# Output projections of the first two tiles start earlier, and the work at the seam of two phases is put in another order

## The reference

```
x = x + layernorm(attention(layernorm(x)))        # causal, 16 heads of 64, rotary on q and k
x = x + layernorm(ffn(layernorm(x)))
attention: q, k, v = x Wq, x Wk, x Wv ; out = softmax(mask(q k^T) / 8) v ; out Wo
ffn:       scores = 8 softmax(x Wr^T + br) ; low = x A^T (8 experts, rank 16)
           out = 2 * sum over experts of scores * (low B^T)
```

## Time and profile before

| | us |
|---|---|
| median of three runs | 1061.37 |
| lowest and highest of the runs | 1061.04, 1061.68 |
| the profiled execution, own time | 1061.38 |
| its span, first to last instruction | 1059.6 |
| mean granted TensorE clock, share of full speed | 0.997 |
| busy: PE, DVE, ACT, POOL | 1037.3, 753.5, 624.0, 421.5 |

### The profile page before, as it was taken

How to read it: one execution, slowest core, us unless ns; L and a number is a source line. 1 busy time by engine, 2 the same in 40 slices (tenths; PEclk the granted TensorE clock), 3 DMA queues, 4 the chain that set the end, 5 groups by cost and what they waited for, 6 DMA issues and landing times.

```text
span 1059.6 us, 19431 instructions
## 1 busy us (share of the span) xinstructions
PE 1037.3 (98%) x6135; PEld 897.5 (85%) x6135; DVE 753.5 (71%) x2170; ACT 624.0 (59%) x1454; POOL 421.5 (40%) x422
## 2 busy tenths in 40 slices
PE   7999999999999999999999999999989999999996
PEld 6988888888888888888888888888877888888884
DVE  8576777777676667667766766676766777777777
ACT  7567666767665666566665756666685333333334
POOL 5143524443362536245342624444367232333221
PEclk9999999999999999999999999999999999999999
DMA  7013323331320247011111101110342323332311
GB/s 298 21 65 110 110 71 110 110 110 51 96 73 27 92 161 249 21 51 50 55 51 50 54 13 51 51 51 16 100 159 62 119 81 100 119 104 88 105 61 60
DMA packets 58699, 90.83 MB, mean 86 GB/s; under 512 B 3568, under 2 KB 36336, under 8 KB 58608
## 3 DMA queue, kind: packets, MB, share of 16 engines
q1 hardware_dynamic: 58464, 89.44, 26.3%
q10 hardware_dynamic: 144, 0.26, 0.1%
HBM read 64.52 MB, written 25.17 MB: 85 GB/s over the span
## 4 chain that ended last, share of the span: by engine, by line
PE 80%; DVE 6%; ACT 5%; issue 5%; POOL 1%; DVEq 0%; ACTq 0%; POOLq 0%
PE bank L1523 26%; PE bank L1468 24%; PE bank L1550 14%; PE bank L1582 5%; PE bank L1602 3%; PE bank L1601 2%; PE bank L1720 2%; PE bank L1697 1%; DVE prob L1121 1%; ACT prob L805 1%; ACT q_hl L826 1%; PE bank L1721 1%; ACT xin L787 1%; ACT pT L816 1%; ACT xn L769 1%
## 5 line engine op out<-in xcount | busy, mean ns | idle before, releaser
L653 POOL TENSOR_SCALAR prob<-prob,rinv 128x128 f32<-128x128 f32 (+3 forms) x256 | 137.5, 537 | 442.2 <-DVE rinv L1131 442.2
L805 ACT ACTIVATE prob<-prob,nmax 128x128 f32<-128x128 f32 (+3 forms) x256 | 144.3, 564 | 231.9 <-DVE nmax L1121 230.0
L1523 PE MATMUL bank<-big_hi,w_hi 128*128 128x512 f32 (+1 forms) x520 | 217.2, 418 | 0.6 <-DVE big_lo L1096 0.3
L1523 PE MATMUL bank<-big_hi,w_lo 128*128 128x512 f32 (+1 forms) x520 | 203.3, 391 | 0.0
L1523 PE MATMUL bank<-big_lo,w_hi 128*128 128x512 f32 (+1 forms) x520 | 202.3, 389 | 0.0
L1121 DVE CUSTOM_DVE_ANT_0 prob<-bank,mask 128x256 f32<-128x256 f32 (+2 forms) x192 | 106.2, 553 | 64.5 <-PE bank L1468 63.2
L1550 PE MATMUL bank<-wv_hi,big_hi 128*128 128x256 f32 x512 | 132.9, 293 | 0.0
L1550 PE MATMUL bank<-wv_hi,big_lo 128*128 128x256 f32 x512 | 127.2, 281 | 0.0
L1139 DVE TENSOR_TENSOR pT<-bank,pT 128x128 fp32r<-128x128 f32 (+3 forms) x256 | 124.3, 486 | 1.6 <-ACT pT L816 1.4
L1582 PE MATMUL bank<-ident,prob 128*128 128x128 f32 x640 | 111.9, 273 | 5.2 <-DVE pT L1139 3.4
L1523 PEld LDWEIGHTS bank<-big_hi,w_lo 128*128 128x128 f32 x520 | 97.6, 188 | 21.6
(11 more groups left out here) (159 smaller groups left out, 2281.0 us busy)
## 6 DMA issues: line engine op xcount, KB each, us to landing
w_raw<-in_wqkv SPq DMA_DIRECT2D x32, 512.0 KB, 4.5
wv_raw<-in_wqkv SPq DMA_DIRECT2D x16, 512.0 KB, 4.5
attention_out<-o_sum SPq DMA_DIRECT2D x64, 128.0 KB, 2.3
w_raw<-attention_out SPq DMA_DIRECT2D x16, 512.0 KB, 4.8
land<-in_x SPq DMA_DIRECT2D x16, 512.0 KB, 3.7
out<-res SPq DMA_DIRECT2D x14, 512.0 KB, 2.7
xin<-in_x SPq DMA_DIRECT2D x12, 512.0 KB, 4.0
xT_hold_hi<-xin SPq DMA_DIRECT2D x8, 512.0 KB, 3.6
```

What stands on the lines that cost most here:

```text
L653: pool.tensor_scalar(p, p, rinv[:, q % 4:q % 4 + 1], 1.0, ALU.mult, ALU.mult).then_inc(prob_done, 1)
L805: act.activation(prob[:, q % 4, 0:n], prob[:, q % 4, 0:n], ACT.Exp, scale=-1.0, bias=nmax[:, q % 4:q % 4 + 1], accum_out=rsum[:, q % 4:q % ...
L1523: done = pe.matmul(grp_ps[k][:, cols], w, xt[:, cols], start=at == 0, stop=at == GROUP_MM - 1)
```

## The change

- The chunks of tile 0 begin two steps earlier (`Y_FIRST_AT`: slot 31, step 6), and tile 1 begins in slot 32, step 6 instead of slot 33, step 0; twelve of its chunks instead of eight stand inside the slots. Half 0 of tile 1 goes to the bank `tr_ps`, which the v projections used (`y_bank`), and the transposes of the first half of tile 0 to `sc_ps[0]`. The waits follow the banks.
- ScalarE: `oT_high(0)` a step later, Wo chunk 4 a step later and chunk 5 two steps later, `oT_high(2)` a step later, the first `ln_start` of tile 0 two steps earlier, the second ahead of the last `o_lower`.
- GpSimd: `oT_low(0)` a step later; Wo chunks 5, 6 and 7 a step earlier; `oT_low(1)` two steps earlier; `bt_lo` behind `chunk_sums`. In all slots, the first `w_pairs` moves from step 1 of the odd slot to step 3 of the even slot ahead of it, and `wv_low` comes a step earlier.
- VectorE: `y_variance(0)` moves from slot 33, step 1 to slot 32, step 7, ahead of the last `negate`; the first sums and statistics of x1 from step 3 to step 2; the low part of the second half of tile 0 ahead of the copy of the column sums.
- TensorE: `columns` moves behind the first chunk of tile 2.

```
--- before.py
+++ after.py
...
 CHUNKS = 8
-Y_FIRST = (((0, 0), (0, 1), (0, 2)), ((0, 3), (0, 4)), ((1, 0), (1, 1)), ((1, 2), (1, 3)), ((1, 4), (0, 5)),
-           ((1, 5),), ((0, 6), (1, 6)), ((0, 7), (1, 7)))
-Y_SECOND = ((0, 1), (2, 3, 4), (5, 6, 7))
+Y_FIRST = (((0, 0), (0, 1)), ((0, 2), (0, 3)),
+           ((1, 0), (1, 1), (1, 2)), ((1, 3), (0, 4)), ((1, 4), (0, 5)), ((1, 5), (0, 6)), ((1, 6),), ((0, 7), (1, 7)))
+Y_SECOND = (((0, 0), (0, 1)), ((0, 2), (0, 3)), ((0, 4), (0, 5)), ((0, 6), (0, 7), (1, 0)), ((1, 1), (1, 2), (1, 3)))
 WO_EARLY = UPH - 2
 WO_SLOT = STEPS * (UNITS - 2)
-WO_AT = {STEPS * WO_EARLY + 4: 0} | {WO_SLOT + s: c for s, c in ((4, 1), (9, 2), (10, 3), (12, 4), (13, 5), (16, 6), (17, 7))}
-WO_POOL_AT = {STEPS * WO_EARLY + 6: 0} | {WO_SLOT + s: c for s, c in ((6, 1), (9, 2), (10, 3), (13, 4), (16, 5), (17, 6), (18, 7))}
+Y_FIRST_AT = STEPS * UNITS - 2
+Y_SECOND_AT = Y_FIRST_AT + len(Y_FIRST)
+WO_AT = {STEPS * WO_EARLY + 4: 0} | {WO_SLOT + s: c for s, c in ((4, 1), (9, 2), (10, 3), (13, 4), (15, 5), (16, 6), (17, 7))}
+WO_POOL_AT = {STEPS * WO_EARLY + 6: 0} | {WO_SLOT + s: c for s, c in ((6, 1), (9, 2), (10, 3), (13, 4), (15, 5), (16, 6), (17, 7))}
 EARLY = TILES // 2
...
-            if isinstance(t, int) and t == 0 and k == 1:
-                return pt_ps[0]
+            if isinstance(t, int) and t == 0:
+                return pt_ps[0] if k == 1 else sc_ps[0]
             return grp_ps[0] if final(t) and k == 1 else tr_ps
+
+        def y_bank(t, i, k):
+
+            return tr_ps if isinstance(t, int) and t == 1 and k == 0 else y_ps[i][k]
...
                     divide(u, s)
-                    if u % QUAD == QUAD - 1 and u < UNITS - 1 and s in (3, 4):
-                        wv_low(u // QUAD + 1, s - 3)
-                    if b == 1 and not (isinstance(u, int) and u >= UNITS - 1):
-                        if s in (1, 6):
-                            w_pairs(s // 6, n + 1)
+                    if u % QUAD == QUAD - 1 and u < UNITS - 1 and s in (2, 3):
+                        wv_low(u // QUAD + 1, s - 2)
+                    if b == 0 and u < UNITS - 2 and s == 3:
+                        w_pairs(0, n + 1)
+                    if b == 1 and u < UNITS - 1:
+                        if s == 6:
+                            w_pairs(1, n + 1)
                         if s in (5, 7):
                             w_low(s // 7, n + 1)
-                    if isinstance(u, int) and STEPS * u + s == STEPS * UNITS - 5:
+                    if u == UNITS - 1 and s == 4:
                         oT_low(0, 0)
-                    if isinstance(u, int) and u == UNITS and s in (4, 5):
-                        oT_low(1, 1, PART * (s - 4), PART * (s - 3))
+                    if u == UNITS and s in (2, 3):
+                        oT_low(1, 1, PART * (s - 2), PART * (s - 1))
                     if isinstance(u, int) and u == UNITS + 1 and s == 2:
                         oT_low(2, 0)
-                    if isinstance(u, int) and u == UNITS + 1 and s == 3:
-                        pool.wait_ge(bt_hi_done, 1)
-                        pool.tensor_tensor(bt_lo, bt_raw, bt_hi.bitcast(F32), ALU.subtract).then_inc(bt_lo_done, 1)
                     if isinstance(u, int) and STEPS * u + s in WO_POOL_AT:
...
             chunk_sums()
+            pool.wait_ge(bt_hi_done, 1)
+            pool.tensor_tensor(bt_lo, bt_raw, bt_hi.bitcast(F32), ALU.subtract).then_inc(bt_lo_done, 1)
             for t in range(2, 6):
...
                         x_normal(ahead_tile(u) + 1)
-                    if isinstance(u, int) and u == UNITS - 1 and s in (3, 6):
-
+                    if u == UNITS - 1 and s in (4, 6):
                         act.wait_ge(grp_done, 2 * u + s // 3)
...
                     if isinstance(u, int) and u == UNITS + 1:
-                        if s == 1:
+                        if s == 2:
                             oT_high(2, 0, 32)
-                        if s == 2:
+                        if s == 0:
                             ln_start(ln_first(0))
...
                             act.activation(ar_hi, ar_raw[:, :, :], ACT.Copy).then_inc(ffn_hi_done, 1)
+                            ln_start(ln_second(0))
                             o_lower(u - 2, 1)
-                        if s == 4:
-                            ln_start(ln_second(0))
                     if isinstance(u, int) and u == UNITS and s == 5:
...
                         hold_chunk(u, HOLD_AT.index(s), half, ahead)
+                    if u == UNITS and s == 7:
+                        y_variance(0, 0)
                     if isinstance(u, int) and u == UNITS + 1:
-                        if s == 1:
-                            y_variance(0, 0)
-                        if s == 3:
-                            dve.memset(br_sb[:, 0:HR], 0.0).then_inc(br_zeroed, 1)
-                            dve.memset(ones[:, :], 1.0).then_inc(ones_set, 1)
+                        if s == 2:
                             y_scale(0, 0)
...
                             ln_variance(ln_second(0))
+                        if s == 3:
+                            dve.memset(br_sb[:, 0:HR], 0.0).then_inc(br_zeroed, 1)
+                            dve.memset(ones[:, :], 1.0).then_inc(ones_set, 1)
                             o_add(u - 2, 1)
...
                         dve.wait_ge(res_done, t - 1)
-                dve.scalar_tensor_tensor(out=x1_of(t, i)[:, half(k)], in0=y_ps[i][k][:, :], scalar=rs1[:, 0:1],
+                dve.scalar_tensor_tensor(out=x1_of(t, i)[:, half(k)], in0=y_bank(t, i, k)[:, :], scalar=rs1[:, 0:1],
                                          in1=xres[:, i, half(k)], op0=ALU.mult, op1=ALU.add
...
             x2T_low(0, 0)
+            x2T_low(0, 1)
+            dve.wait_ge(y0_done, 1)
+            half_stats(0, y_bank(1, 1, 0)[:, :])
             dve.wait_ge(col_done, 1)
...
             low_base(0)
-            x2T_low(0, 1)
-            dve.wait_ge(y0_done, 1)
-            half_stats(0, y_ps[1][0][:, :])
             for t in range(2, 6):
...
                     if isinstance(t, int) and t == 0:
-                        pe.wait_ge(rot_done, 2 * UNITS)
+                        pe.wait_ge(rot_done, 2 * UNITS - 1)
                     pe.wait_ge(oT_hi_done, t + 1)
...
                     if isinstance(t, int) and t == 1:
-                        pe.wait_ge(neg_done, STEPS * UNITS - 1)
+                        pe.wait_ge(v_hi_done, 2 * UNITS)
+                        pe.wait_ge(v_lo_done, 2 * UNITS)
                     if late(t, 2):
                         pe.wait_ge(x1_done, t - 1)
+                if isinstance(t, int) and t == 0 and k == 1 and c0 == 0:
+                    pe.wait_ge(rot_done, 2 * UNITS)
                 if isinstance(t, int) and t == 1 and k == 1 and c0 == 0:
...
                     cols = slice(512 * k, 512 * k + 512)
-                    last = products(y_ps[i][k][:, :], [(oT_hi[:, i, c, :], wo_hi[c][:, cols]),
+                    last = products(y_bank(t, i, k)[:, :], [(oT_hi[:, i, c, :], wo_hi[c][:, cols]),
                                                        (oT_lo[:, i, c, :], wo_hi[c][:, cols]),
...
-                    if isinstance(u, int) and STEPS * u + s in range(STEPS * UNITS, STEPS * UNITS + len(Y_FIRST)):
-                        for k, c in Y_FIRST[STEPS * (u - UNITS) + s]:
+                    if STEPS * u + s in range(Y_FIRST_AT, Y_SECOND_AT):
+                        for k, c in Y_FIRST[STEPS * u + s - Y_FIRST_AT]:
                             y_half(0, 0, k, c, c + 1)
-                    if isinstance(u, int) and u == UNITS + 1 and s < len(Y_SECOND):
-                        for c in Y_SECOND[s]:
-                            y_half(1, 1, 0, c, c + 1)
+                    if STEPS * u + s in range(Y_SECOND_AT, Y_SECOND_AT + len(Y_SECOND)):
+                        for k, c in Y_SECOND[STEPS * u + s - Y_SECOND_AT]:
+                            y_half(1, 1, k, c, c + 1)
...
                 if isinstance(t, int) and t == 0 and k == 0:
-                    pe.wait_ge(v_hi_done, 2 * UNITS)
-                    pe.wait_ge(v_lo_done, 2 * UNITS)
+                    pe.wait_ge(neg_done, STEPS * UNITS)
                 elif isinstance(t, int) and t == 0:
...
                 y_half(t, i, 0, 0, 1)
+                if isinstance(t, int) and t == 2:
+                    columns()
                 low_rank(t - 2)
...
-            y_half(1, 1, 1, 0, 4)
+            y_half(1, 1, 1, 4, 6)
             x2_turn(0, 0, 0)
-            y_half(1, 1, 1, 4, 6)
-            columns()
+            y_half(1, 1, 1, 6, 7)
             x2_turn(0, 0, 1)
-            y_half(1, 1, 1, 6, KC)
+            y_half(1, 1, 1, 7, KC)
             for t in range(2, 6):
...
```

## The result

The changed kernel takes 1064.73 us (median; 1064.28 to 1066.09), the kernel before 1061.37 (1061.04 to 1061.68): ratio 1.0035, 95% interval 1.0025 to 1.0045. It is slower, by 3.4 us. The forecast was 1062.6, the range 1058.4 to 1065.4. The time lies inside the range, but outside the forecast's own narrower one (1061.2 to 1063.8): what came is the second rival on top of the forecast, at 1064.8.

What follows compares the result with a forecast made beforehand. TensorE was taken as the bound (busy 1037 of 1060 us), VectorE's chain close behind. Gains in slot 31 are given back in four waits, `low_turn` comes later: 1061.4 + 1.3 = 1062.6 us, rounded; range 1058.4 to 1065.4.

Steps and rivals of the forecast that it cites:

- second rival: Behind `oT_low(2)`, `bt_lo` comes first and blocks `ar_lo`, which ends 2.2 us later: 1064.8 us; chance 0.24.
- sum of +1.3 us: At the first `low_turn`: it starts at 830.8 against 829.47, and the delay is carried to the end.
- Slot 31: Four chunks of tile 0 fill the 2.17 us gap after a 0.8 us wait; later transposes start at 786.5, not 786.09.
- Slots 0 to 30 at nothing (-0.3 to +0.5): Moving `w_pairs` and `wv_low` there stays within GpSimd's idle share: 0 us, range -0.3 to +0.5.
- GpSimd in slot 32: `divide` queues behind `wo_low(5)`; TensorE waits 1.6 and 1.4 us, and item 1's transposes start 2.0 us later.
- VectorE's order: `y_variance` (1.7 us) ahead of the last `negate`, which starts 3.1 us late; VectorE is free for x1 1.7 us late.
- a race: After the last `pt_low`, `bt_lo` starts 5.6 us behind it and `ar_lo` is ready 5.7 us behind it.
- a fall of the clock in slot 32: Gaps of 1.6, 0.6 and 0.8 us there bring half speed, costing 1.7 us: 1064.3 us; chance 0.08.
- To the end: Behind `low_turn` the order of turns is unchanged, so the 1.3 us is carried to the end.
- Rival 1: In slots 31 and 32 the divisions keep ahead of TensorE and the lead survives: 1059.3 us; chance 0.28.

Runs made afterwards that it cites:

- e1: The changed kernel with only `bt_lo` on GpSimd moved from behind the column sums to slot 32, step 6; 1062.51 us.
- e8: The kernel before with only the edits of slots 0 to 30 (`w_pairs` and `wv_low`); 1060.85 us, ratio 0.9994.
- e3: e1 with `y_variance` and the first `ln_start` put back behind the last `negate`; 1061.69 us.
- e6: The changed kernel with the edits of e1, e3, e5 and e11 together; 1059.84 us, ratio 0.9984.
- e10: e6 with `chunk_sums` ahead of `oT_low(2)` in slot 33; 1059.34 us, ratio 0.9982.
- e5: The changed kernel with ScalarE's copies of Wo chunks 4 and 5 one and two steps earlier, GpSimd's subtraction of chunk 5 one step earlier; 1064.50 us.
- e12: e10 with `bt_lo` moved back from slot 32 to behind `oT_low(2)`; 1061.36 us.
- e7: e6 with tile 0 beginning in slot 32, step 0 again, and tile 1 two steps later; 1062.48 us.
- e2: e1 with the low parts of Wo chunks 5, 6 and 7 put back one step later on GpSimd; 1061.99 us.
- e11: The changed kernel with the last `o_lower` ahead of the second `ln_start` on ScalarE; 1061.77 us.

## Why the forecast was right in its parts and wrong in its choice

The forecast's own steps came, and its sum of +1.3 us held (1.38 in the seam of e1). It failed by leaving out the clash that it had named as its second rival, and the price of that rival held too. The time lies in the wide range because the range reached over this rival, not because the forecast expected it.

- **Slot 31.** Right. `y_half` began at 781.56 after 0.63 us of waiting (forecast 0.8), `q_low` took 1.82 us, and the transposes of item 5 started at 785.71. That is 0.8 us ahead of the forecast, because TensorE came out of slots 0 to 30 earlier by 0.76 (last projection 779.86, before 780.62). The next steps carry the same lead.
- **Slots 0 to 30 at nothing (-0.3 to +0.5).** Off: about -0.5 (e8), outside its bounds, by the profiles; the interval of e8's ratio alone doesn't exclude no change. The rows from 400 to 779 us, which show no gap, were taken for all the slots. Between 40 and 240 us TensorE stands idle for 1.94 us in before, and there e8 closes 0.3 us.
- **GpSimd in slot 32.** Right. `wo_low(5)` took 2.90 us beside `k_low`, `divide` of item 7 stood behind it, and TensorE waited 1.40 us (forecast 1.6), then another 0.98 (forecast 1.4). The transposes of item 1 came at 798.54 (forecast 799.4).
- **VectorE's order.** Right. `y_variance` (808.45) went ahead of `negate` (810.31, forecast 811.2), and the last `pt_low` ended at 815.02 (forecast 815.7): less the lead, within 0.15 us. e3 gives the place of `y_variance` a price of 0.7 to 0.8 us.
- **`ar_lo`.** Here the forecast failed. It put the start of `bt_lo` 5.6 us and that of `ar_lo` 5.7 us behind the last `pt_low`, and called it a race. Measured from its end (815.02) they are at 5.39 and 5.92. By the forecast's own numbers `bt_lo` was ahead, by 0.1 us; yet it gave that case 0.24 and made its sum with the other. Nothing in the rows was set against those two numbers; the trace of before, in which `ar_lo` was never second, was no evidence for the new order.
- **The price of rival 2.** 2.2 us, which e1 confirms (1064.73 - 1062.51 = 2.22), but made of other parts. `ar_lo` lost 1.70 us, not 2.2, as `bt_lo` had already run for 0.53 us when `ar_lo` came (0.1 in the forecast). The other 0.5 came from the clock: behind the 3.22 us gap `low_rank` and six chunks took 832.35 - 824.66 = 7.69 us instead of 6.0 (1.85 + 4.15), so TensorE, not `wlow` (done 831.79), set `low_turn`. The forecast had looked for a fall of the clock in slot 32, where none came.
- **To the end.** Right: 230.1 to 230.2 us from `low_turn(0)` in every profile.

That the total came within 0.1 us of the rival's 1064.8 is in part luck: the clock's 0.5 us, which the sum didn't have, stands against the 0.5 us that it had too much for `ar_lo`.

The sum as measured in the profile: 1.38 (the steps of the seam, e1) + 2.26 (what the clash added, 1.7 by `ar_lo` and 0.5 by the clock) - 0.76 (ahead of the seam in this execution) = 2.88, the difference of the spans. The medians differ by 3.4: the profiled execution was the fastest of the changed kernel's seven.

Rival 1 (the lead survives, 1059.3) was right that `divide` behind `wo_low(5)` decides, but its price was too high. e6 and e10 reach 1059.8 and 1059.3 only with more edits, of `y_variance` and `o_lower`. An estimate for the lead alone, from e5: `wlow` ends 50.48 us into the seam there, of which 1.71 are `ar_lo`'s loss; without it `low_turn` would stand at 48.8, as in before, so 1.4 us less than e1 and not 3.3. Three waits for GpSimd, of 0.31, 0.65 and 0.80 us, stay in e5; how much of the difference is theirs no run shows.

## What to carry to other kernels

Filling idle time on the bounding engine moves the demand on all the others: here the 3.3 us of idle time filled came back as four waits for GpSimd (3.2 us) and one of 1.5 us for VectorE (e1), and the clash of `bt_lo` and `ar_lo` added 2.2 us. Before an order is changed, find the first instruction behind which nothing differs any more (here `low_turn(0)`) and make the sum to it. Where a VectorE instruction with two SBUF operands and a long GpSimd instruction come within a microsecond of each other, write down both starts, and if the margin is smaller than what the sums are good for, separate the two: the one on the path must not be second, and moving `bt_lo` into slot 32 took the whole 2.2 us away (e1).

## What the runs showed of the hardware that was not expected

- A gap of 2.31 us (e12) lowered the granted clock to half speed in the profiled run, and so did two gaps of 1.77 and 1.90 us close together (e7). Gaps of 1.54 and 1.48 us (e1, e2) didn't, nor did 1.40, 0.34 and 0.64 in slot 32 (after). Behind gaps of equal length the low stretch differs: after (3.22 us) 0.61 over 4.4 us, e5 (3.25 us) 0.57 over 8 us. Nor does a shorter gap mean a shorter stretch: e12 stays at 0.50 from 824 to 828. What sets its length stays open.
- The GpSimd instruction waits too when it is second: `wo_low` 2.90 instead of 2.40, `ar_sum` 1.40 instead of 0.47 (e6), `bt_lo` 3.43 instead of 2.35 (e11). A long duration of a GpSimd row may be a wait for VectorE; the bracket ahead of the row doesn't show it.
